# Post-norm decoder, two layers: second feed-forward layer of a sequence in two halves over three steps instead of one piece over two

## What is computed

```python
def _L0_ffn_ref(x, w1, conv_w, conv_b, w2):
    h = bit_linear(x, w1)                 # 256 -> 1024, activations rounded per row
    h = depthwise_conv1d(h.transpose(0, 2, 1), conv_w, conv_b)   # 3 taps
    h = jax.nn.silu(h.transpose(0, 2, 1))
    return bit_linear(h, w2)              # 1024 -> 256, activations rounded per row
...
x = _layernorm(x + _L0_ffn_ref(x, ...), axis=-1)
x = _layernorm(x + _L1_attn_ref(x, ...), axis=-1)   # one head of 256, softmax over the queries
```

## Time and profile before

| | us |
|---|---|
| median of 3 runs | 2614.4 (2607.5 to 2623.3) |
| profiled execution: time | 2618.6 |
| its span | 2616.6 |
| PE busy | 2127.3 (81%) |
| VectorE busy | 1468.5 (56%) |
| ScalarE busy | 1190.2 (45%) |
| POOL busy | 675.5 (26%) |
| third stage, first to last matmul | 1513.8 to 2094.2 |

### The profile page before, as it was taken

How to read it: one execution, slowest core, us unless ns; L and a number is a source line. 1 busy time by engine, 2 the same in 40 slices (tenths; PEclk the granted TensorE clock), 3 DMA queues, 4 the chain that set the end, 5 groups by cost and what they waited for, 6 DMA issues and landing times. The chain is left out here.

```text
span 2616.6 us, 32649 instructions
## 1 busy us (share of the span) xinstructions
PE 2127.3 (81%) x11586; PEld 1188.9 (45%) x11586; DVE 1468.5 (56%) x2771; ACT 1190.2 (45%) x2631; POOL 675.5 (26%) x750
## 2 busy tenths in 40 slices
PE   3688888888888689999999723789899947788786
PEld 1334344344343346565655512456566723445454
DVE  3546456455565266666666457484835315557655
ACT  1154543544545255555555255566642224353342
POOL 4610220221010200000000056464632032442223
PEclk7799999999999899999999956899999968899898
DMA  7423342352321200000000110010000056543311
GB/s 159 126 58 67 76 84 57 78 96 59 60 53 34 68 19 5 19 15 20 17 7 9 37 41 17 1 39 11 25 26 11 17 132 121 131 95 80 75 52 41
DMA packets 127859, 139.77 MB, mean 53 GB/s; under 512 B 35933, under 2 KB 102369, under 8 KB 127602
## 3 DMA queue, kind: packets, MB, share of 16 engines
q1 hardware_dynamic: 127698, 137.69, 22.8%
HBM read 99.16 MB, written 38.47 MB: 53 GB/s over the span
## 5 line engine op out<-in xcount | busy, mean ns | idle before, releaser
L512 ACT ACTIVATE pbuf_sb<-psB 128x512 f32<-128x512 f32 (+1 forms) x608 | 330.8, 573 | 328.6 <-PE psB L394 305.6
L679 DVE TENSOR_REDUCE negm_sb<-psA 128x1 f32<-128x768 f32 (+6 forms) x352 | 347.4, 1022 | 159.8 <-PE psA L382 157.1
L1036 ACT ACTIVATE pw_sb<-psA,nmx_sb 128x154 f32<-128x154 f32 x512 | 192.0, 387 | 194.4 <-DVE nmx_sb L1127 194.4
L391 PE MATMUL psB<-qst_sb,kst_sb 99*128 99x512 bf16 (+3 forms) x768 | 234.2, 335 | 43.0 <-ACT pbuf_sb L512 34.8
L380 PE MATMUL psA<-kst_sb,qst_sb 96*128 96x512 bf16 (+3 forms) x768 | 200.7, 341 | 27.4 <-DVE negm_sb L679 25.0
L1127 DVE TENSOR_REDUCE nmx_sb<-psA 128x4 f32<-128x616 f32 x128 | 102.2, 799 | 176.6 <-PE psA L904 176.6
L408 PE MATMUL psO<-pbuf_sb,V_sb 128*32 128x512 f32 (+3 forms) x1536 | 169.2, 514 | 8.8 <-ACT OT_sb L498 7.4
L2483 DVE TENSOR_REDUCE negm_sb<-psA 128x2 f32<-128x320 f32 x256 | 116.0, 480 | 82.4 <-PE psA L2152 81.0
L2310 ACT ACTIVATE pb_sb<-psB 128x512 f32<-128x512 f32 x160 | 92.8, 600 | 142.9 <-PE psB L2162 140.6
L391 PEld LDWEIGHTS psB<-qst_sb,kst_sb 99*128 99x128 bf16 x768 | 74.7, 98 | 180.2 <-ACT pbuf_sb L512 146.4
L1076 POOL TENSOR_SCALAR std_sb<-mv_sb 128x1 f32<-128x1 f32 x32 | 7.3, 228 | 503.4 <-DVE mv_sb L1154 503.4
(11 more groups left out here) (265 smaller groups left out, 4495.2 us busy)
## 6 DMA issues: line engine op xcount, KB each, us to landing
qst_sb<-parts_dram SPq DMA_DIRECT2D x192, 128.0 KB, 4.4
rden_sb<-dens_dram SPq DMA_DIRECT2D x128, 128.0 KB, 2.7
parts_dram<-parts_sb SPq DMA_DIRECT2D x32, 384.0 KB, 2.5
kst_sb<-parts_dram SPq DMA_DIRECT2D x96, 128.0 KB, 7.2
x_dram<-X_sb SPq DMA_DIRECT2D x64, 128.0 KB, 1.7
parts_dram<-partsb_sb SPq DMA_DIRECT2D x16, 384.0 KB, 2.9
xT_sb<-xT SPq DMA_DIRECT2D x4, 1024.0 KB, 5.2
X_sb<-x SPq DMA_DIRECT2D x4, 1024.0 KB, 5.2
```

Of the source, the lines that this page charges most:

```text
L391: last = nc.tensor.matmul(psB[:, k, at:at + hi - lo], kst[0:MAX_ROWS, gg % 3, h, i * P:(i + 1) * P], qst[0:MAX_ROWS, gg % 3, h, lo:hi], st ...
L512: nc.scalar.activation(pbuf[:, key % 2, heads[0]:heads[-1] + 1, lo:hi], psB[:, (nb.n - 1) % 2, 0:len(heads) * (hi - lo)] .rearrange("p (h ...
L679: nc.vector.tensor_reduce(out=negm[:, gg % 2, heads[0]:heads[-1] + 1, j], in_=psA[:, (na.n - 1) % 2, :].rearrange("p (h n) -> p h n", h=le ...
L1036: last = nc.scalar.activation(pw[:, m % 2, h, :], psA[:, m % 2, at:at + K], ACT.Exp, bias=nmx[:, m % 2, h:h + 1], accum_out=psx[:, m % 3, ...
```

## The change

Tiles 0 to 3 of the second layer, with their residuals, inverse deviations and normalisations, stay in step 5; tiles 4 to 7 go to step 6. Pairs 0 and 1 of the transposes stay in step 6, and pairs 2 and 3 go to step 7, each pair ahead of the projections of its step. This is done on all four engines and in the numbering of the banks. The lag of two tiles between residual and normalisation starts anew in each half. quantise_x, scale_x and everything else stay at their places, and no instruction is added or dropped.

```diff
--- before.py
+++ after.py
@@ -1290,13 +1290,12 @@
         if m == 0 and tile_at(s) is not None:
             for j in range(4, NT):
                 number_c(("v", tile_at(s) // NT, j))
-        if m == 5 and e is not None:
-            for j in range(NT):
+        if m in (5, 6) and e is not None:
+            for j in range(4 * (m - 5), 4 * (m - 4)):
                 number_c(("w2", e, j))
         if m in (6, 7) and e is not None:
-            if m == 6:
-                for i in range(NT // 2):
-                    number_t(("xt", e, i))
+            for i in range(2 * (m - 6), 2 * (m - 5)):
+                number_t(("xt", e, i))
             for qk in ("k", "q"):
                 for c in range(KC):
                     number_c((qk, e, c, m - 6))
@@ -1484,13 +1483,12 @@
                 if m == 0 and tile_at(s) is not None:
                     for j in range(4, NT):
                         project_v(tile_at(s) // NT, j)
-                if m == 5 and e is not None:
-                    for j in range(NT):
+                if m in (5, 6) and e is not None:
+                    for j in range(4 * (m - 5), 4 * (m - 4)):
                         second_layer(e, j)
                 if m in (6, 7) and e is not None:
-                    if m == 6:
-                        for i in range(NT // 2):
-                            transpose_x(e, i)
+                    for i in range(2 * (m - 6), 2 * (m - 5)):
+                        transpose_x(e, i)
                     for qk in ("k", "q"):
                         for c in range(KC):
                             project_qk(qk, e, c, m - 6)
@@ -1599,9 +1597,8 @@
                     for j in range(4, NT):
                         copy_v(tile_at(s) // NT, j)
                 if m in (6, 7) and e is not None:
-                    if m == 6:
-                        for i in range(NT // 2):
-                            copy_xt(e, i)
+                    for i in range(2 * (m - 6), 2 * (m - 5)):
+                        copy_xt(e, i)
                     for qk in ("k", "q"):
                         for c in range(KC):
                             copy_qk(qk, e, c, m - 6)
@@ -1801,13 +1798,14 @@
                     copy_rows(tile_at(s))
                 if chunk_at(s - 2) is not None:
                     take_max(chunk_at(s - 2))
-                if m == 5 and e is not None:
-                    for j in range(NT):
-                        if j >= 2:
+                if m in (5, 6) and e is not None:
+                    first = 4 * (m - 5)
+                    for j in range(first, first + 4):
+                        if j >= first + 2:
                             normalise_hidden(e, j - 2)
                         residual(e, j)
-                    normalise_hidden(e, NT - 2)
-                    normalise_hidden(e, NT - 1)
+                    normalise_hidden(e, first + 2)
+                    normalise_hidden(e, first + 3)
                 if s % 8 == 6 and f is not None:
                     scale_x(f)
                 if tile_at(s - 2) is not None:
```

## The result

The changed kernel takes 2639.7 us (median of 7 runs, 2628.5 to 2642.2), the kernel before beside it 2617.7 (7 runs, 2607.5 to 2623.3): a ratio of 1.0078, 95% interval 1.0054 to 1.0103. That is slower by 20 to 22 us where +20.0 was forecast. Its profiled execution took 2639.7 us, with a span of 2637.7.

The account below looks back on a forecast made before the run. PE (TensorE) was taken as the bound. Sequences 0 to 3 summed 11.9 + 8.3 + 0.4 - 0.6 = +20.0 us, on the median 2614.4 + 20.0 = 2634.4 us, with a range from 2618 to 2648.

Parts of the forecast that it names:

- POOL's queue: Step 6, sequences 0 and 1: inverse deviations wait behind quantisation, starting the first key projection +4.75 and +3.0 us later.
- ScalarE's queue: Step 7, sequence 0: copies of pairs 2 and 3 stand behind outer_taps, delaying the projection by +5.15 us.
- the third term: Step 7, sequences 1 to 3: transposes wait for the bank and projections for the second copy, +3.0 us each.
- The two transposes without cover: Step 7, sequences 1 to 3: pairs 2 and 3 no longer cover a copy, so PE waits, +3.0 us each.
- Residual waits: PE's waits for VectorE's residuals over the third block fall from 8.5 to about 4 us.
- The clock: PE drops to half clock behind new long gaps: +0.65 and +2.5 us in sequence 0, +2.3 in sequence 1.
- The three clock terms: Half-clock charges in sequences 0 and 1, 5.45 us together; may be nothing or cost 2.7 us each.
- Rival (1): Sequences' steps 5 to 7: same waits, but the clock doesn't pay; +14.5 us, 2629; chance 0.15.
- Rival (2): POOL lets go early: quantisation at 11.2 us, half of ScalarE's 5.15 shows; +11 us, 2625; chance 0.2.
- Rival (3): Waits for residuals and late copies vanish if tile 4's inverse deviation reaches VectorE before residual 5's done; 2596; chance 0.05.
- rival (4): Held VectorE delays taps, silu and later second layers, or each new gap costs 3 us of clock; +30, 2645; chance 0.15.

Follow-up runs that it names:

- e2: The changed kernel with ScalarE's copies of pairs 2 and 3 put ahead of silu and outer_taps in step 7 of sequence 0: 2640.0 us, 1.0084 of the kernel before.
- e6_both: The changed kernel with POOL's quantisation split over steps 5 and 6, and transpose pairs 2 and 3 behind step 6's projections: 2606.1 us, 0.9974 of the kernel before.
- e1: The changed kernel with POOL's quantisation in two halves, rounds 4 to 7 behind step 6's inverse deviations: 2626.4 us, 1.0049 of the kernel before.
- e4: The kernel before with only transpose pairs 2 and 3 moved to step 7, all eight tiles left in step 5: 2635.1 us, ratio 1.0074.

## Why the prediction was right, point by point

The four terms, from the start of the second layer (k6, k7 are the key projections of steps 6 and 7, v the value projections):

| | start to k6 | k6's own, longer | else up to k7 | k7 to v | sum |
|---|---|---|---|---|---|
| seq. 0 forecast | +4.75 | +0.65 | +5.15 | +1.33 | +11.9 |
| seq. 0 measured | +4.88 | +0.99 | +5.16 | +0.22 | +11.25 |
| seq. 1 forecast | +3.0 | +2.3 | +3.0 | 0 | +8.3 |
| seq. 1 measured | +3.62 | +2.82 | +3.10 | +0.10 | +9.64 |
| seq. 2 forecast | -2.6 | 0 | +3.0 | 0 | +0.4 |
| seq. 2 measured | -2.73 | +0.10 | +3.10 | +1.81 | +2.28 |
| seq. 3 forecast | -3.6 | 0 | +3.0 | 0 | -0.6 |
| seq. 3 measured | -3.80 | +0.10 | +3.10 | +1.79 | +1.19 |

- **POOL's queue.** Right in place, chain and size: the quantisation was put at 13.0 us in sequence 0 and took 13.0; in sequence 1 it took 13.4, which is 0.4 of the 0.6 missing there. VectorE's waits, said to be some 8 us, were 10.7 and 8.0, and in sequences 2 and 3 none is over 0.8. PE stood 8.0 us in sequence 0 as said, and 7.6 for "nearly 6" in sequence 1, since it also came to the wait 1.0 us earlier than reckoned. By the Trainium skill, page "SBUF — State Buffer", section "Who interferes with whom", a residual, with one input in PSUM, leaves POOL alone; the trace agrees. Beside the residual at 1650.33 the two quantising instructions took 0.86 and 0.48 us, where with VectorE idle they take 0.85 and 0.48. The first one, beside the middle tap, took 1.40.
- **ScalarE's queue.** Right: +5.15 forecast, +5.16 measured. With the queue out of the way (e2) 3.4 of it go; 1.8 stay, the two pairs of transposes (1.06 us) and the wait for their copy (0.74), the same as the third term in the other sequences.
- **The two transposes without cover.** Right: +3.10 in all three sequences for +3.0.
- **Residual waits.** Right in step 5's part: the short ones fell from 8.5 us to 4.2 (about 4 was said). But the wait of 7.82 us ahead of tiles 6 and 7 in sequence 0 is for a residual too. The prediction had residual 4 as late as it was (about 1648, measured 1649.25 with all 1.3 us later) and didn't name the wait; it stands where that of 10.3 us for the copy stood.
- **The clock.** This term was mis-sized. "The three clock terms (5.45)" left sequences 2 and 3 at nothing; the shortest gap with a fall behind it that the prediction had read was 2.94 us. In sequences 2 and 3 it fell behind gaps of 1.13 and 0.74 us with transposes between, and cost 1.8 in each. Sequence 1's gap cost 2.8 for 2.3, sequence 0's second one 1.6 for 2.5. In all: the forecast is 4.4 us under the measured 24.4, of which 3.6 are the two falls that weren't foreseen.
- **The median.** The 20.0 is met within a microsecond by the ratio (1.0078 of 2614.4 is +20.4). That is partly luck: the third stage lost 4.4 more than forecast, and in the trace 3.3 of it were made good in the parts that the change doesn't touch (4.6 less behind the stage, 1.3 more ahead of it).
- **The rivals.** Rival (1), that the clock doesn't pay, is out: 8.0 us of the 24.4 are longer busy time. The Trainium skill, page "TensorE: Matmul & The Clock Gate", Part 1, puts the ramp penalty at less than 1% of a typical kernel's span, and speaks there of the warm-up. In this trace the clock falls again and again: its mean over the execution, 0.917 between the levels 0.5 and 1.0, means that it stood at the lower one for a sixth of the span. So that figure is no ground for leaving the clock out here, where it makes a third of what the change did. Rival (2) is out, with 13.0 and 13.4 us of quantisation for 11.2 and the whole of ScalarE's 5.15. Rival (3), that the waits just vanish, failed on its condition: VectorE waited 10.7 us for POOL. With POOL's order mended and the transposes well placed (e6_both) VectorE still waits 5.1 us for it, and 4.7 us come in, not 18.8: in sequence 0 a wait of 7.9 us for VectorE takes the place of the 10.3. Of the knock-on in rival (4) there is nothing, as the stretches between are the same to 0.04 us, and the new gaps cost 1.0 to 2.8 us of clock each, not 3.

## What to carry to other kernels

When a step is cut in two, follow each queue that its small instructions pass, not only the one of the bound engine: four instructions of 0.9 us behind sixteen others on the least busy engine (26%) cost the bound one the 13.6 us that splitting the sixteen gave back. Work that seems to be filler (transposes between a copy and its reader) may be the cover of that copy; move it only to a place where something else stands between it and its reader, as behind the projections here. And where a change loses, take its parts separately before it is dropped: the two orders that cost were both free to choose, and the rest was a gain, if a small one (4.7 us).

## What was not expected of the hardware

TensorE's clock fell behind two short waits in some executions and not in others, with the same instructions and gaps to 0.01 us ahead of it. Step 7 of sequence 2, the waits and the projections, in the changed kernel and then in e2_copies_first (windows; the clock is the third figure from the end):
```profile
1931.50:1934.50 3.00, 1.13 (x10) 0.87 (x9) 2.55 (x5) 1.68 (x3) 0.77 (x2) 1.00 0.03 5
1934.50:1940.00 5.50, 5.50 (x9) 2.39 (x10) 0.00 (x0) 0.67 (x2) 0.00 (x0) 0.69 0.07 24
```
```profile
1934.40:1937.40 3.00, 1.14 (x9) 0.93 (x9) 2.48 (x5) 1.68 (x3) 0.77 (x2) 1.00 0.00 0
1937.40:1942.90 5.50, 5.50 (x13) 2.50 (x14) 0.00 (x0) 1.32 (x3) 0.00 (x0) 1.00 0.09 27
```
In the first the clock is at 0.69 on average over the projections, so part of them ran at 1.2 GHz, in the second all at 2.4. In the traces of the change, e1, e2 and e4, the pair of waits in step 7 of sequences 1 to 3 occurs twelve times; the projections behind it took 5.40 us six times and 3.70 the other six. The same page of the Trainium skill says of a kernel's start that the activity monitor's window runs freely, so that one kernel's count of slow matmuls varies from run to run; the six and six fit that. What decides it in a given execution stays open here. For a forecast it means that such a pair of waits is worth its own 1.9 us and, in six cases of these twelve, 1.7 more.
